# Attention with row maxima computed ahead: the maxima run 28 tiles ahead of the scores in place of 32

## What is computed

```python
    def _L0_attn_ref(x, w_att_val, wv_w, wv_b, out_w, out_b):
        ...
        x_h = x.reshape(b, t, h, d).transpose(0, 2, 1, 3)
        xw = jnp.einsum('bhtd,hde->bhte', x_h, w_att_val)
        att = jnp.einsum('bhte,bhse->bhts', xw, x_h) / jnp.sqrt(jnp.asarray(d, x.dtype))
        att = jax.nn.softmax(att, axis=-1)
        vx = x @ wv_w.T + wv_b
        vx = vx.reshape(b, t, h, d).transpose(0, 2, 1, 3)
        o = jnp.einsum('bhts,bhsd->bhtd', att, vx)
        o = o.transpose(0, 2, 1, 3).reshape(b, t, e)
        return o @ out_w.T + out_b
    ...
        gate = fp4_linear(x, w_gate)
        y = fp4_linear(x, w_up)
        h = jax.nn.silu(gate) * y
        return fp4_linear(h, w_down)
    x = L0_attn_x
    x = x + _L0_attn_ref(_layernorm(x, axis=-1), L0_attn_w_att_val, L0_attn_wv_w, L0_attn_wv_b, L0_attn_out_w, L0_attn_out_b)
    x = x + _L0_ffn_ref(_layernorm(x, axis=-1), L0_ffn_w_gate, L0_ffn_w_up, L0_ffn_w_down)
```

## Time and profile before

| | us |
|---|---|
| median of 3 runs | 1469.53 |
| lowest, highest | 1469.02, 1470.22 |
| profiled execution, its own time | 1474.33 |
| its span in the trace | 1472.3 |
| mean granted TensorE clock | 0.985 of full |

### The profile page before, as it was taken

The page is one execution under the profiler, slowest core; times in us unless marked ns, Lnnn a source line. Parts: engine busy times, 40 slices in busy tenths (PEclk is TensorE's granted clock), DMA queues, the critical chain, the costliest instruction groups (busy, mean ns, idle before and its releaser), DMA issues. The chain is left out here.

```text
span 1472.3 us, 32419 instructions
## 1 busy us (share of the span) xinstructions
PE 1427.1 (97%) x8612; PEld 892.5 (61%) x8612; DVE 1267.7 (86%) x2648; ACT 868.1 (59%) x1730; POOL 658.3 (45%) x910
## 2 busy tenths in 40 slices
PE   6799999999999999999999998899999999999998
PEld 4355555555555555555555554577777777777776
DVE  6788888888888888888888886699999999999995
ACT  1477777777777777777777776533333334343432
POOL 2346546546546546546546421243434343434341
PEclk8699999999999999999999999999999999999999
DMA  7665455455455455455455461000000000000000
GB/s 208 198 165 167 135 156 167 133 156 166 135 155 169 132 155 170 131 155 170 131 156 157 126 163 37 0 15 18 14 18 14 18 14 18 14 18 14 18 15 22
DMA packets 99785, 148.09 MB, mean 101 GB/s; under 512 B 21024, under 2 KB 58272, under 8 KB 99744
## 3 DMA queue, kind: packets, MB, share of 16 engines
q1 hardware_dynamic: 82672, 137.22, 32.6%
q10 hardware_dynamic: 17072, 10.37, 2.6%
HBM read 85.02 MB, written 65.27 MB: 102 GB/s over the span
## 5 line engine op out<-in xcount | busy, mean ns | idle before, releaser
L1175 DVE TENSOR_REDUCE neg_max<-ring 128x1 f32<-128x512 f32 x1016 | 637.1, 682 | 87.2 <-PE ring L907 81.2
L1058 ACT ACTIVATE probs<-scores 128x512 f32<-128x512 f32 x1024 | 536.8, 601 | 181.7 <-PE scores L918 172.4
L1625 PE MATMUL gu_bank<-splits,f_x_T 128*128 128x352 f32 x1024 | 313.7, 459 | 0.1
L907 PE MATMUL ring<-x_stack,q_stack 64*128 64x512 f32 x1016 | 232.6, 454 | 22.2 <-DVE neg_max L1175 14.0
L940 PE MATMUL ring<-probs,v_quad 128*32 128x512 f32 x2048 | 248.1, 602 | 0.1
L1625 PEld LDWEIGHTS gu_bank<-splits,f_x_T 128*128 128x128 f32 x1024 | 189.6, 190 | 95.4 <-ACT f_x_T L1599 0.5
L915 PE MATMUL scores<-q_stack,x_stack 64*128 64x512 f32 x1024 | 207.0, 398 | 5.1 <-ACT probs L1058 3.4
L907 PEld LDWEIGHTS ring<-x_stack,q_stack 64*128 64x128 f32 x1016 | 98.2, 188 | 175.9 <-DVE neg_max L1175 123.7
L918 PE MATMUL scores<-max_stack,max_ones 64*128 64x512 f32 x1024 | 204.5, 393 | 0.0
L1381 POOL TENSOR_TENSOR f_small<-f_small,eps 128x1 f32<-128x1 f32 x64 | 43.2, 676 | 296.0 <-DVE f_small L1348 296.0
L1584 ACT ACTIVATE h_T<-h_bank 128x512 f32<-128x512 f32 (+1 forms) x128 | 55.8, 487 | 176.3 <-PE h_bank L1635 176.3
(11 more groups left out here) (135 smaller groups left out, 2000.8 us busy)
## 6 DMA issues: line engine op xcount, KB each, us to landing
x_rows<-splits SPq DMA_DIRECT2D x128, 256.0 KB, 3.3
x_stack<-x_rows SPq DMA_DIRECT2D x126, 256.0 KB, 4.0
q_stack<-q_rows SPq DMA_DIRECT2D x248, 128.0 KB, 4.0
q_rows<-splits SPq DMA_DIRECT2D x64, 256.0 KB, 2.2
out_dram<-x_all SPq DMA_DIRECT2D x64, 128.0 KB, 1.7
x_all<-in_L_attn_x_dram ACTq DMA_DIRECT2D x14, 512.0 KB, 3.6
w_raw<-slabs SPq DMA_DIRECT2D x14, 192.0 KB, 4.0
slabs_kept<-w_turned SPq DMA_DIRECT2D x14, 192.0 KB, 4.4
```

Source lines behind the costliest of these rows:

```text
L907: pe.matmul(max_bank(c, q, ROWS * n + m)[:, :], row_tile(q_stack[q], m)[:, p, s * P:(s + 1) * P], row_tile(x_stack[q], m)[:, p, :], start= ...
L1058: act.activation(probs[j][:, k, :], scores[k][:, :], ACT.Exp).then_inc(p_ready, 1)
L1175: dve.tensor_reduce(neg_max[g % 2][:, at:at + 1], tile[:, :], AX.X, ALU.max, negate=True).then_inc(m_used, 1)
L1625: m = pe.matmul(gu_bank[c][:, :], x_T[u][:, a, :], gate_up_T[:, a, c * CH:(c + 1) * CH], start=(a == 0), stop=(a == HALVES - 1))
```

## The change

`BEHIND` = 4 tiles are taken off the lead of the maxima. The lead becomes 28 tiles: quad 0 and the first 12 of quad 1 come ahead of batch 0. In each quad i, step j = 0 now has the last 4 tiles of quad i + 1, and steps 1 to 3 the first 12 of quad i + 2 (`aimed` maps a place in the ring to the tile that is computed there). Since a quad's maxima are complete only after j = 0 of the quad before it, the round trip moves with them: POOL's split from the start of quad i to its step j = 1, the turn on DVE from j = 0 to j = 1 behind the third reduction (`TURN_BEHIND` = 2), ACT's store from behind the exponentials of j = 0 to behind those of j = 1, and ACT's load from between the exponentials of j = 2 to behind them. The first scores come after 28 tiles (`AHEAD` = 6). In the last batch, step (2,0) has 4 max tiles that it had not.

```diff
+    BEHIND = QUAD
...
+    def aimed(g, n, per):
+
+        quads, number = divmod(2 * per + n - BEHIND * per // (QUAD * TT), per)
+        return g + quads, number
...
-    POOL_STEP = {(0, 0): ("maxima", "values0", "halves", "x0"), (0, 1): ("values1",), (0, 3): ("values2", "values3"),
+    POOL_STEP = {(0, 0): ("values0",), (0, 1): ("maxima", "halves", "x0", "values1"), (0, 3): ("values2", "values3"),
...
+    TURN_BEHIND = 2
+
+    AHEAD = 6
+    FIRST_MAXIMA = 2 * QUAD * TT - BEHIND
...
-            for g in range(2):
-                for n in range(PAIRS * TT):
-                    if (g, n) == (1, AHEAD):
-                        pe.wait_ge(pool_set, POOL_SET)
-                        step_scores(0, 0, 0, True)
-                    max_scores(-1, g + 2, n)
+            for n in range(FIRST_MAXIMA // ROWS):
+                if n == PAIRS * TT + AHEAD:
+                    pe.wait_ge(pool_set, POOL_SET)
+                    step_scores(0, 0, 0, True)
+                g, at = divmod(PAIRS * TT * QUADS - FIRST_MAXIMA // ROWS + n, PAIRS * TT)
+                max_scores(-1, g, at)
+            if AHEAD == FIRST_MAXIMA // ROWS - PAIRS * TT:
+                pe.wait_ge(pool_set, POOL_SET)
+                step_scores(0, 0, 0, True)
...
                     exponentials(i, j, first and g == 0,
-                                 (lambda: load_maxima(i + 1, (g + 1) % QUADS)) if loading else None,
                                  (lambda: take(early, b)) if early is not None and stands(early, b) else None)
+                    if j == 1 and not (last and g == 3):
+                        store_maxima(i + 1, (g + 1) % QUADS)
+                    if loading:
+                        load_maxima(i + 1, (g + 1) % QUADS)
                     if j == 0 and not (first and g == 0):
                         end_half(i - 1, (g - 1) % QUADS)
                     if j == 2:
...
-                    if j == 0 and not (last and g == 3):
-                        store_maxima(i + 1, (g + 1) % QUADS)
...
-                        if j == 0 and s == (1 if first and g == 0 else 3) and turning:
+                        if j == 1 and s == TURN_BEHIND and turning:
                             turn_maxima(i + 1, (g + 1) % QUADS, first and g == 0)
```

More of the change, by code:

```diff
@@ L1012, in quad @@
                 start = first and g == 0
-                ahead = not (last and g >= 2)
                 for j in range(TT):
+                    ahead = in_ring(("max", g, QUAD * j), b)
                     if ahead:
@@ L1048, in _, with exponentials @@
         def _(act):
-            def exponentials(i, j, start, between=None, ahead_of_last=None):
+            def exponentials(i, j, start, ahead_of_last=None):
                 for k in range(QUAD):
-                    if k == QUAD // 2 and between is not None:
-                        between()
                     if k == QUAD - 1 and ahead_of_last is not None:
@@ L1298, in batch @@
                     quad(b, g, isinstance(b, int) and b == 0, isinstance(b, int) and b == B - 1)
[L1300 to L1304 removed]
+            for k in range(FIRST_MAXIMA):
+                if k == QUAD * TT:
+                    turn_maxima(0, 0, True)
+                reduce_max(-1, *divmod(QUADS * QUAD * TT - FIRST_MAXIMA + k, QUAD * TT))
             batch(0)
```

46 lines of the change are left out of this document (21 added, 25 removed).

## The result

The changed kernel takes 1481.14 us in the median of 4 runs (1478.57 to 1486.57), the kernel before beside it 1469.88 (1469.02 to 1470.23). The ratio is 1.0072, with a 95% interval from 1.0057 to 1.0086: **slower by 0.7%, some 11 us**, where I had forecast 1.9 us less. The profiled execution after is the slowest of the four, 1486.57 with a span of 1484.6. Its span is 12.3 us over that of before.

A forecast was written before the change was run, and what follows sets the result against it. PE was taken to bound the loop (busy 198.9 of 200 us), the tile-reduction chain the start; -4.4 + 2.5 + 0.3 - 0.6 + 0.3 = -1.9 us, from median 1469.5 to 1467.6, range 1464.0 to 1473.5.

The forecast's parts named there:

- The start: Batch 0: scores of (0,1) 5.1 us earlier, at 46.05; 0.7 given back by the clock; -4.4 in sum.
- DVE in the loop: Turn ahead of the fourth reduction at j = 1: 0.12 us per step (2,1), 0.05 per (0,1), +2.5 in all.
- The round trip: Moved store and load, tight in quad 1: store lands at 403.2 to 403.7, 0 to 0.1 us a batch, +0.3.
- The round trip is late in the loop: Rival: quad 1's store lands at 404.5, copy 0.8 us late for PE each batch, 1479 us; chance 0.18.
- Both signs: Signs of being wrong, in the loop: ACT waits for `max_rows` in every batch; PE waits in quad 1 for `pv_rows`.
- The late stores of quad 2: ACT's four waits for stores, 3.9 us in all, go away; only part had reached PE, so -0.6 (0 to -1).
- The last batch and step (2,0): Last batch: store held by feed-forward weights, 0 (-1 to +1); four max tiles in step (2,0), +0.3.

The follow-up runs named there:

- The run with the load behind the copy: Changed kernel with ACT's load of the maxima put behind the copy `pv_rows` in every quad: 1468.58 us, ratio 0.9980 to the kernel before.
- The run with the late store: Kernel before with only ACT's store of the maxima moved behind the exponentials of j = 1: 1503.06 us, ratio 1.0216.
- the run with the small transfer: Changed kernel, SP's load of quad 0's next operands cut to 32 of 512 columns from batch 1 on: 1469.51 us, ratio 0.9989.
- 30 tiles: Changed kernel with lead shortened by 2 tiles instead of 4, round trip left as in the kernel before: 1497.31 us, ratio 1.0156.
- the load alone was moved: Kernel before with only ACT's load of the maxima moved behind the exponentials of j = 2: 1469.85 us, ratio 0.9988.

## Why the prediction was wrong

**The start: right.** Forecast -5.1 for the scores of (0,1) and 0.7 back for the clock, -4.4 in all. Measured 46.85 in place of 46.05, because (0,0) started 0.74 later (its load landed later; this differs from run to run, from 40.16 to 41.75). The clock rose at 54.5, 5.4 us earlier than before, so here it took nothing back, and batch 1 started 4.69 us earlier. Two things in this are luck. The working tied the rise to PE's last pause, and the other traces don't bear that out. The run with the load behind the copy starts with the same instructions, and its clock rose at 49.1, ahead of the end of its last pause (0.81 us, ended at 50.49). The run with the late store starts as the kernel before, and its clock rose at 54.6, ahead of the pause that ended at 55.58 (columns as in the earlier trace rows):

```profile
48.00:50.00 2.00, 1.68 (x10) 0.78 (x6) 1.16 (x4) 1.63 (x4) 0.00 (x0) 0.72 1.15 340
54.00:56.00 2.00, 1.22 (x8) 0.91 (x9) 1.16 (x2) 1.25 (x3) 0.48 (x1) 0.85 0.94 274
```

And the start of batch 1 lies between 97.9 and 101.7 in the seven traces with a lead of 28, and between 102.6 and 104.3 in the three that start as before, so one pair of traces can't tell 4.4 from 4.69.

**DVE in the loop: right.** Forecast 0.05 and 0.12 us in (0,1) and (2,1), 2.5 in all. Measured 0.09 in each, 2.2 in 13 batches (the sum right, the two sizes less so), and gone when the turn goes behind the fourth reduction. What I missed is that the turn's place also decides whether ACT's issue of the store is covered; that would have cost 13 us if the change had put it elsewhere.

**The round trip: the step that failed.** I wrote of the store in quad 1: "So it drains at about 402.9 and lands at 403.2 to 403.7", and took +0.3 for it. It landed at 404.88, which is 404.3 in the time of before, and the term is **+15.1** (and 0.7 more in batch 14). What failed is the time from the drain to the landing: I had 0.3 to 0.8 us, and it took 2.4. The rival "The round trip is late in the loop" is what happened, nearly to the number: a landing at 404.5, the copy at 405.1 (405.07 in the time of before), 0.8 us a batch (1.16 in the mean), 1479 (1481). I gave it 0.18.

From the earlier trace rows I took that a transfer of ACT goes behind what SP has issued, and counted bytes. The earlier trace rows alone is weak evidence. The load issued at 401.68 in the kernel before had its first packet at 403.41, 1.7 us later; the load in the run with the small transfer, with nothing in its way, had it 0.9 us later (398.38 to 399.31). So half of that silence was the ordinary time from issue to first packet. But the single packets of the other runs bear the reading out as far as the store's first packet. Medians over 13 batches, in us and KB ("ahead" is what SP had issued and not yet moved when the store was issued; "same bytes moved" is when SP had moved as many):

| store | ahead, KB | same bytes moved | issue to first packet | first to last packet | last packet to landing | in all | SP's KB beside it, and behind it until it landed |
|---|---|---|---|---|---|---|---|
| before, quad 1 | 348 | 0.99 | 1.20 | 0.36 | 0.40 | 1.96 | 0, 0 |
| after, small transfer, quad 1 | 32 | 1.93 | 1.20 | 0.36 | 0.40 | 1.96 | 0, 16 |
| after, quad 1 | 512 | 2.55 | 2.38 | 1.53 | 0.92 | 4.75 | 372, 204 |
| before, quad 2 | 1079 | 3.18 | 3.17 | 1.18 | 0.43 | 4.69 | 228, 0 |
| 30 tiles, quad 2 | 1388 | 4.63 | 4.46 | 1.42 | 0.40 | 6.40 | 274, 0 |

(The medians of the parts and of the whole are each their own.) The first packet comes 1.20 us behind the issue, or when little is left of what SP had issued before (60 KB of the 512 in the median), whichever is later. Of the 882 stores in the 14 traces 314 have it later than 1.35 us, and by then SP had moved 90% of those bytes in the median (75% to 109% in nine of ten). One store fits badly: in batch 14 of the run with the small transfer, where the load is whole, 512 KB stood ahead and the first packet came at 1.43, with 280 of them still to move; SP issued its next load 1.0 us behind that store, elsewhere 0.3. So it is a regularity of these traces and not a proven mechanism, and what in the chip makes the first packet wait no run shows. The drain that I forecast, 2.67 us behind the issue, is about right by it: 512 KB stood ahead in place of 640, and the first packet came at 2.38.

The store is not done by then, and this is what I priced at 0.3 to 0.8 us. SP issues 512 KB more from 0.33 us behind the store on, and their packets move beside it. In the same window as the earlier trace rows the packets of the queues, after:

```profile
q1 hardware_dynamic: 149, 0.46, 95.7%
q10 hardware_dynamic: 116, 0.01, 5.7%
```

ACT's queue (q10) moves 116 packets while SP's (q1) moves 149. The rule of the Trainium skill that I had set aside ("DMA: Bandwidth & Descriptors", "Queues, rings and completion order": each DMA engine goes round-robin between its queues, a packet at a time) agrees with this part; of a wait for the first packet it says nothing. So 128 small packets took 1.53 us in place of 0.36. The landing comes 0.92 us behind the last packet, not 0.40. The same section says that the write that counts up the semaphore "lands only after every earlier write from that SDMA engine, across its queues", so that it also has SP's writes ahead of it; the trace agrees as far as it goes, since the two stores of quad 2, behind whose last packet SP moved nothing more, landed 0.43 and 0.40 us behind it. Neither rule gives a time by itself; a row of a small store amid such a transfer would have, and the earlier trace rows pointed to four of them, in quad 2, that I priced by their wait and not by their landing (4.69 us behind the issue, by the table above).

Both signs that I had named came: ACT waits for `max_rows` in every batch, and PE in quad 1 for `pv_rows`.

**The late stores of quad 2: small, as forecast.** Forecast -0.6; the waits of the earlier trace rows are gone, and (2,3) gained 0.1 (0.8 where the load alone was moved).

**The last batch and step (2,0): step (2,0) right, the batch outside its bounds.** From the scores of (1,3) to those of (2,1) the last batch took 5.58 us in place of 5.30, 0.28 more, forecast 0.3. The batch and all behind it gave 1.5 back, in steps (0,3) and (1,0), forecast 0 with 1 to either side; the trace of before has 6.8 us at half clock there and that of after 3.4, so I can't tell an effect of the change from the clock.

In sum, by the profiled executions: -4.7 at the start, +17.7 in batches 1 to 13, +0.8 in batch 14, -1.5 in the last, 12.3 in all. Without the one term it would be a small gain, and with the load behind the copy it is one: 2.9 us under the kernel before.

## What to carry to other kernels

A wait on an engine's queue costs what is behind it, so put the instruction that waits for a DMA behind everything that another engine needs soon; here the order of two calls was worth 0.9% of the kernel. Before a small store is moved, look at which large transfer will be under way at its new place, and take its landing from a row with the same traffic. The bytes to drain gave the time of its first packet here and no more; what is issued behind it counts too. And when a step of one engine is delayed, follow it through the queues to the transfers it triggers: POOL's wait of 3.5 us in quad 1 cost 1.2 us a batch in quad 2, by way of SP and ACT.

## What the runs showed of the hardware

- A store of 16 KB in 128 packets landed 1.96 us after its issue where SP's queue had emptied by its first packet (quad 1 of the kernel before), and 4.2 to 5.6 us amid a megabyte of that queue. By the medians above 1.2 us more pass before the first packet, 1.2 more from first to last, and 0.5 more between the last packet and the semaphore.
- In most stores the first packet came when SP's queue had moved nearly what it had issued before the store, and not before 1.19 us: 348 KB ahead 1.20 us, 512 KB 2.38, 1079 KB 3.17, 1388 KB 4.46. Behind it the packets of both queues mix (116 of ACT's beside 149 of SP's).
- An issue of a DMA on ACT (0.56 us) doesn't delay ACT's work if it is reached while the instruction ahead of it still runs, and delays the next by 0.5 us if it has to wait for its condition first (`o_T`, 0.52 <-issue).
- The granted clock rose at 59.9 and 59.2 in two traces that start as the kernel before and at 54.6 in the third, and between 43.1 and 54.5 in the seven with a lead of 28. So it differs by 5 to 11 us between traces of the same start, and what it goes by these runs don't show. Behind a pause of 1.66 us in the loop (batch 8 after) it fell to half.
